# TensorE's register loads in a window-building stage: 16-bit numbers, 32 bytes for a batch, limits apart

## The reference

```
h = max(layernorm(x), 0)
agg = segment_sum(edge_weight[:, None] * h[src], dst, num_segments=3125)
h = (h + agg) @ W + b          # then layer norm, gelu; twice; then a projection
```

## Time and profile before

| what | value |
|---|---|
| median of three runs | 3085.93 us (3084.87 to 3090.36) |
| the profiled execution's own time | 3084.36 us |
| its span | 3082.6 us |
| TensorE (PE) busy, whole span | 2588.9 us, 84% |
| VectorE (DVE) busy | 2350.3 us, 76% |
| window stage, 66 to 566 us: PE busy | 356.48 us |
| window stage: DVE busy | 457.39 us |
| window stage: ScalarE (ACT) busy | 373.96 us |
| mean granted TensorE clock in it | 0.87 |

### The profile page before, as it was taken

The page is one execution under the profiler, slowest core; times in us unless marked ns, Lnnn a source line. Parts: engine busy times, 40 slices in busy tenths (PEclk is TensorE's granted clock), DMA queues, the critical chain, the costliest instruction groups (busy, mean ns, idle before and its releaser), DMA issues.

```text
span 3082.6 us, 51075 instructions
## 1 busy us (share of the span) xinstructions
PE 2588.9 (84%) x18059; PEld 1968.9 (64%) x18059; DVE 2350.3 (76%) x3097; ACT 1274.2 (41%) x3089; POOL 1000.1 (32%) x1235
## 2 busy tenths in 40 slices
PE   5677767799989999989599999787777777757999
PEld 3666666454545555479588888565555556646888
DVE  7999999689633444488899999987777777666886
ACT  7777777202000111200255555465555554204443
POOL 3000000011110222303177777677777772011000
PEclk8888888899999999999799999899999999758999
DMA  4434344633447777334288888688877882432553
GB/s 142 167 155 172 159 163 162 239 113 120 127 138 251 254 265 258 119 105 126 73 233 228 233 226 229 167 233 217 217 217 217 217 217 92 139 88 70 167 164 103
DMA packets 311100, 538.18 MB, mean 175 GB/s; under 512 B 108482, under 2 KB 213460, under 8 KB 310596
## 3 DMA queue, kind: packets, MB, share of 16 engines
q1 hardware_dynamic: 241700, 309.63, 30.6%
q0 software_dynamic: 69152, 225.28, 25.7%
HBM read 420.89 MB, written 115.11 MB: 174 GB/s over the span
## 4 chain that ended last, share of the span: by engine, by line
PE 66%; DVE 21%; issue 5%; ACT 4%; DMA 2%; POOL 1%; DVEq 0%; POOLq 0%; SPq 0%; ACTq 0%
PE ps L1658 25%; PE ps L1444 15%; PE ps L1646 9%; DVE a L565 5%; PE ps L1579 5%; DVE a L560 3%; PE ps L1411 3%; PE ps L1357 2%; DVE a L561 2%; PE ps L1577 2%; DVE a L801 1%; PE ps L1413 1%; PE ps L1414 1%; PE ps L1470 1%; DVE a L833 1%
## 5 line engine op out<-in xcount | busy, mean ns | idle before, releaser
L1767 POOL DMA_INDIRECT a<-t,mid x502 | 483.2, 963 | 282.0 <-issue 143.6
L1444 PE MATMUL ps<-a 128*128 128x512 f32 x1200 | 557.4, 604 | 13.2 <-DVE a L742 13.2
L1658 PE MATMUL ps<-a,oh 128*128 128x260 f32 x2008 | 488.1, 390 | 79.0 <-issue 43.1
L1326 ACT ACTIVATE oht<-iota,mid 128x128 f32<-128x128 f32 x830 | 333.3, 402 | 441.0 <-PE ps L1658 399.1
L1658 PEld LDWEIGHTS ps<-a,oh 128*128 128x128 f32 x2008 | 366.5, 191 | 181.0 <-issue 85.1
L1411 PE MATMUL ps<-a 128*128 128x200 bf16 x1568 | 346.0, 277 | 143.5 <-DVE a L560 67.1
L1658 PE MATMUL ps<-wts,oh 128*128 128x260 f32 x1312 | 321.0, 393 | 59.3 <-ACT oh L1328 30.7
L1444 PEld LDWEIGHTS ps<-a 128*128 128x128 f32 x1200 | 219.3, 192 | 221.8 <-issue 215.3
L1137 DVE TENSOR_TENSOR a<-a,ps 128x1040 f32<-128x1040 f32 x251 | 309.6, 1234 | 55.6 <-DMA a<-t,mid 53.1
L1767 POOL DMA_INDIRECT wts<-t,mid x328 | 311.1, 949 | 111.0 <-issue 94.7
L1717 POOL TENSOR_SCALAR rstd<-mv 128x1 f32<-128x1 f32 x75 | 30.2, 403 | 955.7 <-DVE mv L452 953.5
(11 more groups left out here) (325 smaller groups left out, 3946.8 us busy)
## 6 DMA issues: line engine op xcount, KB each, us to landing
a<-at_d SPq DMA_DIRECT2D x60, 1280.0 KB, 6.2
at_d<-a SPq DMA_DIRECT2D x49, 800.0 KB, 3.4
mt_d<-a SPq DMA_DIRECT2D x49, 800.0 KB, 5.6
a<-mt_d SPq DMA_DIRECT2D x30, 1280.0 KB, 6.1
a<-trlo_d SPq DMA_DIRECT2D x49, 512.0 KB
ot_d<-a SPq DMA_DIRECT2D x49, 320.0 KB, 6.0
a<-ot_d SPq DMA_DIRECT2D x49, 256.0 KB, 3.0
a<-t,mid POOLq DMA_INDIRECT x502, 3.8
```

The source lines that it names most:

```text
L1326: e.activation(oht[:, k, :], iota[:, :], ACT.Abs, bias=ndl[:, k, s:s + 1]).then_inc(*own.inc())
L1444: m = e.matmul(acc[f].rearrange("p (x d) -> p x d", x=8), X[:, hi, P * f:P * (f + 1)], a, start=(hi == 0), stop=end, skip_group_check=True)
L1658: t = e.matmul(pbig[b][:, 512 * u:512 * u + 260], oh[:, so, k, :], hrows[2 * r + k][:, 260 * u:260 * (u + 1)], start=(k == 0), stop=(k == 1))
L1767: e.indirect_dma_start(out=hrows[2 * r + k], out_offset=None, in_=t2, in_offset=bass.IndirectOffsetOnAxis(ap=srci[:, k, s:s + 1], axis=0)) ...
```

## The change

The table of column numbers and that of the limits become two tables of 16-bit numbers, `at_tab` (128 for each of 13 partitions) and `at_free` (16 for each). A batch's 16 column numbers are loaded in one register load of 16 x 2 = 32 bytes. The limits are now one for every eight slots, that of the eighth slot, and eight of them are loaded at once, for four batches (64 slots). TensorE waits on `window_free` every eight slots instead of every four. The registers are freed and taken anew at each load.

```
-        at_tab = sb("at_tab", [NSL, P // SB, SB + SB // 4], I32)
+        at_tab = sb("at_tab", [NSL, P], U16)
+        at_free = sb("at_free", [NSL, 16], U16)
...
-            e.tensor_copy(at_tab[:, :, 0:SB], bank(4)[0:NSL, 0:P].rearrange("p (b s) -> p b s", s=SB)).then_inc(*V.inc())
-            e.tensor_copy(at_tab[:, :, SB:], bank(4)[0:NSL, P + 3:2 * P:4].rearrange("p (b s) -> p b s", s=SB // 4)).then_inc(*V.inc())
+            e.tensor_copy(at_tab[:, :], bank(4)[0:NSL, 0:P]).then_inc(*V.inc())
+            e.tensor_copy(at_free[:, :], bank(4)[0:NSL, P + 7:2 * P:8]).then_inc(*V.inc())
...
-            regs = []
+            breg, freg = [], []
             for s in range(S):
                 b, i = divmod(s, SB)
+                k, w = divmod(s, P)
+                if s % 64 == 0:
+                    for r in freg:
+                        e.free_register(r)
+                    freg = [e.alloc_register(f"pf{s}_{n}") for n in range(8)]
+                    e.load(freg, at_free[k:k + 1, w // 8:w // 8 + 8])
+                if s % 16 == 0:
+                    for r in breg:
+                        e.free_register(r)
+                    breg = [e.alloc_register(f"pb{s}_{n}") for n in range(16)]
+                    e.load(breg, at_tab[k:k + 1, w:w + 16])
                 if i == 0:
-                    k = s // P
-                    for r in regs:
-                        e.free_register(r)
-                    regs = [e.alloc_register(f"pb{b}_{n}") for n in range(SB + SB // 4)]
-                    e.load(regs, at_tab[k:k + 1, s % P // SB, :])
                     e.wait_ge(*V("weighted", b))
-                if i % 4 == 0:
-                    e.wait_ge(window_free, e.snap(regs[SB + i // 4], donate=True, min_val=1, max_val=NPAIR + 8))
-                c = e.snap(regs[i], donate=True, min_val=0, max_val=7 * 512 + W2)
+                if i % 8 == 0:
+
+                    e.wait_ge(window_free, e.snap(freg[s // 8 % 8], donate=True, min_val=1, max_val=NPAIR + 8))
+                c = e.snap(breg[s % 16], donate=True, min_val=0, max_val=7 * 512 + W2)
```

More of the change, by code:

```diff
@@ L7 @@
 I32 = mybir.dt.int32
+U16 = mybir.dt.uint16
 BF16 = mybir.dt.bfloat16
```

## The result

The changed kernel takes 3430.29 us in the median of four runs (3426.55 to 3435.49), the kernel before 3085.72 beside it: a ratio of 1.1114, with a 95% interval of 1.1100 to 1.1128. It is 345 us slower where I forecast 39 us faster.

A forecast was written before the change was run, and what follows sets the result against it. TensorE was taken to bound the window stage through load gaps and clock falls; shorter loads would bring it to VectorE's pace, 38.5 us off 3084.36, giving 3046, or 3047 us as the runs' median. Range 3041 to 3076.

The forecast's parts named there:

- What bounds the kernel: Window stage: TensorE, through register-load gaps (143 us) and the lower clock (52 us); 499 us against VectorE's 464.
- The price of a 16-bit load: Batch load of 16 half-words: one price per register whatever its width, 1.10 us in quiet, 2.91 beside the writes.
- The upper bound: Batch load in the window stage: every 16-bit read costs 179 ns, quiet too, so 2.91 us for all.
- The slower rival: Window stage loads: a half-word read costs 179 ns also in quiet, 86 us more, 3170 us; chance 0.07.
- The Trainium skill's figure: Register loads: about 200 ns per register even in bulk; by it, some 120 us slower.
- the quiet row of 68 ns: Kernel before's 20-word load while DMA moved nothing: 68 ns a word, held against a dear 16-bit read.
- The limits' load: 25 new loads of eight limits, every fourth batch: 0.57 us each, quiet side, 0.28 us for every two batches.
- The coarser waits: TensorE's waits on window_free, half as many and for a later bank: cost zero.
- Casts and arithmetic: Two casts before the stage where two stood, slot arithmetic the same: nothing.
- The sum: Two batches on TensorE: 8.6 us at full clock, 0.7 less than 9.32; TensorE ends 39 us earlier.
- part of the gain: Rival for the window stage: clock keeps falling or writes meet more loads, 3052 to 3079 us; chance 0.14.
- the floor: VectorE's pace in the window stage, 4.73 us for each of 98 batches: TensorE ends at 527.3 us.

The follow-up runs named there:

- e8: Kernel before plus a third write of 800 KB after every eight node pairs: 3331.45 us, 43 slower than before on a slower chip.
- e6: e1 with each batch's 16 words loaded in four loads of four words: 3250.94 us, ratio 0.9877 to the kernel before, on a slower chip.
- e3: e1 with the 32-bit column numbers eight bytes apart: 3607.15 us, 318 slower than the kernel before on a slower chip.
- e4: e1 with each load starting four bytes behind a multiple of 16 bytes: 3609.55 us, 321 slower than the kernel before on a slower chip.
- e1: Changed kernel with both tables as 32-bit numbers again: 3264.56 us, ratio 0.9922 to the kernel before, on a slower chip.
- e11: e1 with waits on cleared banks every four slots, sixteen limits in a load: 3055.58 us, ratio 0.9903 to the kernel before.
- e5: Changed kernel with column numbers loaded as 8 32-bit words and split by TensorE's sequencer, limits 32-bit: 3259.26 us, ratio 0.9910 to the kernel before, slower chip.

## Why the prediction was wrong

**What bounds the kernel: right.** The stage was TensorE's, by gaps for register loads that the profile writes against other engines, by the writes beside every second one, and by the clock that falls after a long gap. e8 shows the writes' part. e6 bears out the clock's: it spreads the gaps and gets back the clock and 13 us. It moves both at once, so it doesn't price the clock alone.

**The price of a 16-bit load: the step that failed.** "I take the price as one per register whatever its width, the nearest reading." Two rows, 4 words and 20 words, made a line of 66 ns a register. Both loads happened to be words in a row from a multiple of 16 bytes, and the line was one of trips in disguise: 1, 2, 4 and 5 trips take 0.33, 0.59, 1.10 and 1.36 us, so 0.257 each and 0.07 fixed. A half-word is a trip of its own, 0.233 us. The load went from 5 trips to 16, plus 8 for the limits at every fourth batch: 18 for a batch, against 5.

**The upper bound: too low as well.** I bounded a 16-bit read by 179 ns, the price per word beside the writes, though nothing tied a quiet trip to it. The slower rival rested on that bound and gave 86 us. Measured were 233 ns in quiet, and up to 6.6 us for sixteen beside the writes. The rival also left the clock where it was; its fall to 0.72 is 97 of the 349 us. The bound should have come from dividing a load by the trips that it could consist of, one in the 4-word row: 305 ns. Sixteen numbers would then have cost up to 4.9 us, and the range would have held a large loss.

**The Trainium skill's figure** (Runtime: NRT & Kernel Launch, Instruction fetch mechanics), about 200 ns a register even in bulk, was set aside for the quiet row of 68 ns. The same page of the Trainium skill has this load bring registers from HBM, and here they come from SBUF, so its figure was no sure guide either way. For numbers that don't come 16 bytes at a time the runs agree with it within a fifth: 233 ns for half-words in quiet, and 237 for the words of e3 and e4. It doesn't hold for the aligned words that the kernel before loads. The figure was near for the changed kernel and wrong for the row that I weighed it against. My estimate from it, 120 us slower, had the sign and a third of the size, as it left out the writes and the clock.

**The limits' load: wrong in size and side.** I put it at 0.57 us on the quiet side; it takes 1.92, and in the changed kernel it stands ahead of a long load, as at 301.1 us. As whole words it does take 0.59 (e1). **The coarser waits: right**, no gap is theirs (e1, e11). **Casts and arithmetic: right**, the slot arithmetic stayed at 37 ns.

**The sum, had the price been right: partly.** e1 has the quiet load of the forecast, 1.10 us, and gained 24 us, not 39. VectorE hardly waited (6.1 us), yet TensorE still trailed it: the long loads averaged 3.23 us and not 2.91, and the clock stayed at 0.88, where I had it rise to 0.95 or more. That is the rival "part of the gain". e6 then reached the floor.

## What to carry to other kernels

Before the type or layout of a table that a sequencer loads is changed, count the trips of the load, not its bytes or registers: aligned 32-bit words in a row came at the price of four to a trip; half-words, words apart and words off the 16 bytes came one to a trip. A straight line through two rows says nothing of a case with another type or stride; measure one load of the new kind first. And where an engine's gaps are long because one load is long, cutting it into pieces can be worth more than making it smaller (e6 against e5), even if the pieces aren't hidden, since what fell in e6 was the longest gap.

## What the runs showed of the hardware that I had not expected

- A register load from SBUF: 0.257 us for each 16 bytes of aligned, contiguous 32-bit words (4, 8, 16, 20 words: 0.33, 0.59, 1.10, 1.36 us). Sixteen words eight bytes apart take 3.79 us, sixteen shifted by four bytes 3.80, sixteen half-words 3.78.
- Beside writes from SBUF to HBM a trip takes two to three times as long: of e6's 392 one-trip loads, 130 took over 0.5 us, with a mean of 0.86.
- Shorter loads don't shrink in proportion there. The mean of every second load fell only from 3.54 us (before) to 3.23 (e1) with one trip of five gone; why a trip costs more there, no run shows.
